# Top-k attention: the exponent moves into the evacuations, and GpSimd scales each tile behind its subtraction

## The chip, the core and the metric

The kernel runs on one core of a Trainium2 chip. Its engines work on their own and meet by semaphores: TensorE multiplies matrices (PE in the rows; PEld are its weight loads), VectorE (DVE) and ScalarE (ACT) work element by element, GpSimd (POOL) as well, and SyncE (SP) issues the transfers. The metric is the device time of one execution in microseconds, as the median of several runs.

## What is computed

Two blocks follow each other on an image of 2 x 256 x 48 x 48. The first has an attention of 8 heads of 32 channels over N = 2304 positions, in which each row of scores keeps its 64 largest:

```python
scores = jnp.einsum('bhnd,bhmd->bhnm', q, k) * DHEAD ** (-0.5)
kth = jax.lax.top_k(scores, TOPK)[0][..., -1:]
masked = jnp.where(scores >= kth, scores, jnp.finfo(scores.dtype).min)
attn = jax.nn.softmax(masked, axis=-1)
o = jnp.einsum('bhnm,bhmd->bhnd', attn, v)
```

A projection, a residual and a two-layer network with batch norms come behind it. The second block is a full attention of 8 heads over the same positions, with a projection and a residual. The change is in the first attention alone.

## The kernel before

The first attention (`attention_top`) works on tiles of 128 query rows by 2304 scores. A head has 2 images of 18 tiles; two tiles make a pair, so there are 18 pairs a head and 144 in all. Each engine has its own written program with a loop over heads, and each pair is written out in it; what stands in a program's text is its order, and semaphores are the only links between engines.

A tile goes through these steps. `score` (L366) multiplies queries and keys into PSUM; ScalarE copies the scores to SBUF (`keep_scores`, L449) into one of four slots. VectorE takes the 8 largest of each of 64 chunks of 36 scores (`chunk_tops`, L560). For a pair it then collects extremes and rests (`prepare`, L566 and L577) and finds the 64th largest of each row (`select`, L591 to L624) with the help of a first guess that ScalarE makes (`guess_place`, L480 and L483). `select` and `hand_on` of one pair are woven into the chunks of the next pair's first tile, behind chunks 7 and 19. TensorE counts rows whose threshold is in doubt (`count_doubts`, L393), ScalarE copies the count (`keep_any`, L470), VectorE loads it, searches again where it isn't zero, and hands on the threshold and the row's maximum (`give_kth`, L699 and L700).

ScalarE then writes a penalty into `probs` (`penalty`, L465): zero where a score reaches the threshold, huge where it does not. GpSimd subtracts it from the scores (L542). ScalarE exponentiates the tile in place and sums its rows into `sums` (`exponentials`, L453). TensorE transposes the tile in five groups of up to four 128 x 128 blocks (`turn`, L376) into two PSUM buffers, ScalarE copies each group to SBUF (`keep_turned`, L460), and TensorE multiplies it with the values (`weigh`, L385): 32 columns of values, so four products stand side by side in four bands of 32 rows. ScalarE copies the bands (L525), TensorE adds them up (`add_quadrants`, L404), and ScalarE stores the result (`finish`, L489). `project_out` later divides by the sums. `wait_alone` is a wait with a semaphore step of its own behind it.

## Time and profile before

| | us |
|---|---|
| median of 3 runs | 5078.21 |
| lowest and highest of them | 5076.14, 5078.52 |
| the profiled execution | 5075.16 |
| its span, first to last instruction | 5073.40 |

The profiled execution is one of the same program; its rows give the durations. Times in rows are microseconds from the start of its span, durations marked "mean ns" or "duration ns" are nanoseconds. The first attention fills the span from about 130 to 3230 us. TensorE's clock had a mean of 0.75 of its full rate in that stretch and 0.98 behind it.

### The profile page before, as it was taken

To read this page: it belongs to the slowest core of one execution; us is meant where nothing else is said; L and a number is where in the kernel's file an instruction comes from. 1 tells how busy PE (TensorE), PEld (TensorE's weight loads), DVE (VectorE), ACT (ScalarE), POOL (GpSimd) and SP (SyncE) were. 2 spreads that over 40 slices of the span, in tenths; PEclk is the share of its full clock that TensorE was granted. 3 is DMA by queue.
4 is the path that set the end of the run, shared out by engine and by line. 5 is a ranking of instruction groups with operands and counts; after the bars stand their busy time and mean duration, and the time that the engine had idled before them with its cause. 6 is when DMAs were issued, how large, how long until landed. Compare 5 with 4: busy or idle time off the path is not lost. (4 is left out here: it accounts for less than half of the span.)

```text
span 5073.4 us, 107203 instructions
## 1 busy us (share of the span) xinstructions
PE 4120.5 (81%) x32161; PEld 2777.1 (55%) x32161; DVE 4332.4 (85%) x25624; ACT 4161.6 (82%) x6082; POOL 1502.7 (30%) x362
## 2 busy tenths in 40 slices
PE   8576677777777676777777777898999999999999
PEld 4344445544555444454554445444567777777776
DVE  3999999999999999999999999431378888888886
ACT  2799799999999799999999899544268888888885
POOL 0344445444455444444444444100100000000000
PEclk9777777777777777777777777899899999999999
DMA  6000000000000000000000000200420101111112
GB/s 217 7 18 17 7 17 17 9 17 16 9 18 17 7 17 8 18 18 8 18 18 17 9 17 11 64 6 0 157 73 25 34 25 34 27 32 34 25 34 95
DMA packets 79598, 154.63 MB, mean 30 GB/s; under 512 B 8120, under 2 KB 49464, under 8 KB 73528
## 3 DMA queue, kind: packets, MB, share of 16 engines
q1 hardware_dynamic: 78904, 146.72, 10.1%
q8 instruction: 272, 4.46, 0.4%
q14 instruction: 422, 3.46, 0.2%
HBM read 99.50 MB, written 47.19 MB: 29 GB/s over the span
## 5 line engine op out<-in xcount | busy, mean ns | idle before, releaser
L542 POOL TENSOR_TENSOR a_probs<-a_scores,a_probs 128x2304 f32<-128x2304 f32 x288 | 1460.6, 5092 | 1623.8 <-ACT a_probs L465 1623.8
L560 DVE MAX8 a_top<-a_scores 128x8 f32<-128x36 f32 x18432 | 1832.5, 182 | 31.9 <-ACT a_scores L449 23.4
L376 PE MATMUL a_ps_t<-ident,a_probs 128*128 128x128 f32 x5184 | 964.0, 322 | 521.1 <-ACT a_probs_t L460 378.5
L376 PEld LDWEIGHTS a_ps_t<-ident,a_probs 128*128 128x128 f32 x5184 | 666.7, 163 | 815.0 <-ACT a_probs_t L460 519.6
L1300 DVE TENSOR_SCALAR_CACHE_REDUCE b_soft<-b_ps_s 128x2304 f32<-128x2304 f32 x288 | 735.2, 2553 | 26.2 <-PE b_ps_s L1159 8.5
L465 ACT ACTIVATE a_probs<-a_scores,a_steep_kth 128x2304 f32<-128x2304 f32 x290 | 641.3, 2212 | 136.2 <-DVE a_minus_max L700 136.1
L460 ACT ACTIVATE a_probs_t<-a_ps_t 128x512 f32<-128x512 f32 (+1 forms) x1440 | 728.9, 548 | 14.8 <-PE a_ps_t L376 3.2
L1175 PE MATMUL b_ps_t<-ident,b_soft 128*128 128x128 f32 x5184 | 727.0, 276 | 1.6 <-DVE b_soft_t L1306 0.6
L1175 PEld LDWEIGHTS b_ps_t<-ident,b_soft 128*128 128x128 f32 x5184 | 577.2, 140 | 170.1 <-ACT b_soft_t L1264 60.1
L453 ACT ACTIVATE a_probs<-a_probs,a_minus_max 128x2304 f32<-128x2304 f32 x288 | 638.1, 2216 | 31.8 <-issue 18.1
L366 PE MATMUL a_ps_s<-a_k_stack,a_q_ring 128*128 128x512 f32 (+1 forms) x1465 | 650.8, 604 | 16.1 <-ACT a_scores L449 10.7
L1257 ACT ACTIVATE b_soft<-b_soft,b_minus_max 128x2304 f32<-128x2304 f32 x288 | 638.5, 2217 | 8.2 <-DVE b_soft L1300 8.2
L449 ACT ACTIVATE a_scores<-a_ps_s 128x2304 f32<-128x2304 f32 x292 | 607.1, 2079 | 13.6 <-PE a_ps_s L366 13.6
L385 PE MATMUL a_ps_o<-a_probs_t,a_v 128*32 128x128 f32 x10368 | 568.1, 297 | 0.4
L1264 ACT ACTIVATE b_soft_t<-b_ps_t 128x512 f32<-128x512 f32 (+1 forms) x864 | 422.0, 524 | 166.4 <-PE b_ps_t L1175 166.2
L366 PEld LDWEIGHTS a_ps_s<-a_k_stack,a_q_ring 128*128 128x128 f32 x1465 | 431.3, 318 | 157.0 <-ACT a_scores L449 64.9
L1306 DVE COPY b_soft_t<-b_ps_t 128x512 f32<-128x512 f32 x576 | 393.9, 689 | 80.4 <-PE b_ps_t L1175 80.3
L1159 PE MATMUL b_ps_s<-b_k_stack,b_q_ring 128*128 128x512 f32 (+1 forms) x1440 | 442.9, 405 | 9.7 <-DVE b_soft L1300 5.0
L1136 POOL COPY b_v<-v_all 128x576 f32<-128x576 f32 x16 | 10.7, 670 | 1258.3 <-PE b_ps_o L1194 1153.8
L385 PEld LDWEIGHTS a_ps_o<-a_probs_t,a_v 128*32 128x32 f32 x10368 | 250.8, 112 | 231.8 <-issue 118.2
L404 PE MATMUL a_ps_o<-add_up,a_parts 128*128 128x32 f32 x576 | 146.5, 393 | 276.0 <-ACT a_parts L525 276.0
L1194 PE MATMUL b_ps_o<-b_soft_t,b_v 128*32 128x256 f32 x5184 | 368.4, 384 | 0.6 <-issue 0.6
(133 smaller groups left out, 4135.9 us busy)
## 6 DMA issues: line engine op xcount, KB each, us to landing
a_k_stack<-k_parts SPq DMA_DIRECT2D x72, 288.0 KB, 6.0
b_k_stack<-k_parts SPq DMA_DIRECT2D x72, 288.0 KB, 6.0
a_q_ring<-q_parts SPq DMA_DIRECT2D x294, 64.0 KB
b_q_ring<-q_parts SPq DMA_DIRECT2D x294, 64.0 KB
k_parts<-p_high SPq DMA_DIRECT2D x36, 256.0 KB, 2.0
k_parts<-p_rest SPq DMA_DIRECT2D x36, 256.0 KB, 2.1
q_parts<-p_high SPq DMA_DIRECT2D x36, 256.0 KB, 2.0
q_parts<-p_rest SPq DMA_DIRECT2D x36, 256.0 KB, 2.0
```

Source lines behind the costliest of these rows:

```text
L366: last = pe.matmul(ps_s[:, c:c + n], q_ring[pair % AHEAD_Q][:, P * (s % 2):P * (s % 2) + P], k_stack[b][:, c:c + n], start=True, stop=True)
L376: last = pe.transpose(ps_t[(NTG * s + g) % 2][:, P * m:P * m + P], probs[s % 2][:, P * (m0 + m):P * (m0 + m) + P], cst["ident"][:, :])
L385: last = pe.matmul(ps_o[rows, P * (s % 2):P * (s % 2) + P], v_s[s // MCH][:, m, :], probs_t[:, m, :], start=m < 4, stop=m + 4 >= MCH)
L449: act.activation(scores_all[:, s % 4, :], ps_s[:, 0:N], ACT.Copy).then_inc(scores_kept, 1)
L453: act.activation(probs[s % 2][:, :], probs[s % 2][:, :], ACT.Exp, scale=SCALE, bias=minus_max[parity][:, s % 2:s % 2 + 1], accum_out=sums[ ...
L460: act.activation(probs_t[:, m0:m0 + n, :], ps_t[(NTG * s + g) % 2][:, 0:n * P].rearrange("p (m q) -> p m q", q=P), ACT.Copy).then_inc(turn ...
L465: act.activation(probs[u][:, :], scores_all[:, 2 * parity + u, :], ACT.Relu, scale=-STEEP, bias=steep_kth[parity][:, u:u + 1]).then_inc(pe ...
L542: pool.tensor_tensor(probs[u][:, :], scores_all[:, 2 * (p % 2) + u, :], probs[u][:, :], ALU.subtract).then_inc(masked_ready, 1)
L560: last = dve.max(top8[s // 2 % 2][:, s % 2, c, :], scores_all[:, s % 4, CHUNK * c:CHUNK * c + CHUNK])
L1175: last = pe.transpose(ps_t[(NTG * s + g) % 2][:, P * m:P * m + P], soft[s % 3][:, P * (m0 + m):P * (m0 + m) + P], cst["ident"][:, :])
L1257: act.activation(soft[s % 3][:, :], soft[s % 3][:, :], ACT.Exp, scale=-1.0, bias=minus_max[s % 3][:, 0:1], accum_out=sums[:, s, cols(h + a ...
L1300: dve.tensor_scalar(soft[s % 3][:, :], ps_s[:, 0:N], -SCALE, None, ALU.mult, ALU.min, accum_out=minus_max[s % 3][:, 0:1]).then_inc(shifted ...
```

## The change

The whole-tile exponential (L453) is gone. In its place GpSimd, behind each subtraction, adds the row's negative maximum and multiplies by the scale in a second instruction, with a wait for the subtraction between, and the evacuation of each transposed group computes the exponential in place of a copy. The sums of rows come from TensorE: the values get 32 columns of ones beside their 32, a product has 64 columns, and two stand side by side instead of four. `add_up` has a 33rd column that picks the sum, the result tile keeps 33 columns a head, and `project_out` divides from that tile into one of its own.

The programs of TensorE and ScalarE are written in another order. A tile's groups are turned and weighed in turn; scores of tile s+5 are multiplied behind the first tile's weighing, those of s+6 within the second tile's. ScalarE keeps scores s+5 once the pair's second subtraction is done, and scores s+6 (a new place, at the end of the pair) once the next pair's first subtraction is done.

```diff
-                    rows = slice(D * (m % 4), D * (m % 4) + D)
+                    rows = slice(2 * D * (m % 2), 2 * D * (m % 2) + 2 * D)
...
-                    pe.wait_ge(probs_ready, tile + 1)
+                    pe.wait_ge(shifted_ready, tile + 1)
                     turn(s, 0, tile)
                     turn(s, 1, tile)
-                    score(s + 5, h, tile + 5)
...
+                    for g in range(2, NTG):
+                        turn(s, g, tile)
+                        weigh(s, g - 1, tile)
+                    weigh(s, NTG - 1, tile)
+                    score(s + 5, h, tile + 5)
+                    pe.wait_ge(shifted_ready, tile + 2)
                     turn(s + 1, 0, tile + 1)
-                    weigh(s, 4, tile)
+                    turn(s + 1, 1, tile + 1)
                     count_doubts(pair + 1)
...
-            def exponentials(s, h, tile, parity):
-                act.wait_ge(masked_ready, tile + 1)
-                act.activation(probs[s % 2][:, :], probs[s % 2][:, :], ACT.Exp, scale=SCALE,
-                               bias=minus_max[parity][:, s % 2:s % 2 + 1], accum_out=sums[:, s, cols(h, 1)]
-                               ).then_inc(probs_ready, 1)
...
-                               ACT.Copy).then_inc(turned_kept, 1)
+                               ACT.Exp).then_inc(turned_kept, 1)
...
-                    exponentials(s, h, tile, parity)
-                    keep_scores(s + 4, tile + 4)
+                    exponentials(s, 0, tile)
                     guess_place(1, pair + 1, 1 - parity)
...
+                    for g in range(1, NTG):
+                        exponentials(s, g, tile)
+                    wait_alone(act, masked_ready, tile + 2)
                     keep_scores(s + 5, tile + 5)
                     keep_any(pair + 1)
...
                     guess_place(0, pair + 2, parity)
+                    wait_alone(act, masked_ready, tile + 3)
+                    keep_scores(s + 6, tile + 6)
                     finish(s, h, pair)
...
                     for u in range(2):
-                        pool.wait_ge(penalty_ready, tile + u + 1)
+
+                        wait_alone(pool, penalty_ready, tile + u + 1)
                         pool.tensor_tensor(probs[u][:, :], scores_all[:, 2 * (p % 2) + u, :], probs[u][:, :],
                                            ALU.subtract).then_inc(masked_ready, 1)
+                        wait_alone(pool, masked_ready, tile + u + 1)
+                        pool.tensor_scalar(probs[u][:, :], probs[u][:, :], minus_max[p % 2][:, u:u + 1], SCALE,
+                                           ALU.add, ALU.mult).then_inc(shifted_ready, 1)
...
-                dve.tensor_scalar(minus_max[parity][:, :], extremes[:, :, 0], -SCALE, None,
+                dve.tensor_scalar(minus_max[parity][:, :], extremes[:, :, 0], -1.0, None,
                                   ALU.mult).then_inc(kth_ready, 1)
```

GpSimd, the first pair of a half head, before (`a_probs0` and `a_probs1` are the two tiles of a pair; ISA and REGISTER_ALU are steps of the sequencer):

```order
L538 COPY a_v0<-xs 128x576
L542 ISA
L542 TENSOR_TENSOR a_probs0<-a_scores,a_probs0 128x2304
L541 REGISTER_ALU
L542 TENSOR_TENSOR a_probs1<-a_scores,a_probs1 128x2304
```

and now:

```order
L536 COPY a_v0<-xs 128x18x32
L541 ISA
L541 TENSOR_TENSOR a_probs0<-a_scores,a_probs0 128x2304
L544 TENSOR_SCALAR a_probs0<-a_probs0,a_minus_max0 128x2304
L75 REGISTER_ALU
L541 TENSOR_TENSOR a_probs1<-a_scores,a_probs1 128x2304
L544 TENSOR_SCALAR a_probs1<-a_probs1,a_minus_max0 128x2304
```

Each subtraction has a scale behind it, and the second tile's subtraction comes behind the first tile's scale.

TensorE, from the first tile's last transposes to the count of the doubts, before:

```order
L376 MATMUL a_ps_t<-ident,a_probs 128x128 x2
L385 MATMUL a_ps_o<-a_probs_t,a_v 32x128 x4
L381 REGISTER_ALU
L385 MATMUL a_ps_o<-a_probs_t,a_v 32x128 x4
L430 REGISTER_ALU
L373 ISA
L376 MATMUL a_ps_t<-ident,a_probs 128x128 x4
L381 REGISTER_ALU
L385 MATMUL a_ps_o<-a_probs_t,a_v 32x128 x2
L392 REGISTER_ALU
L393 MATMUL a_ps_o<-a_doubt,ones 1x2
```

and now:

```order
L388 MATMUL a_ps_o<-a_probs_t,a_v 64x128 x4
L384 REGISTER_ALU
L388 MATMUL a_ps_o<-a_probs_t,a_v 64x128 x2
L367 REGISTER_ALU
L369 MATMUL a_ps_s<-a_k_stack,a_q_ring 128x512 x4
L369 MATMUL a_ps_s<-a_k_stack,a_q_ring 128x256
L432 REGISTER_ALU
L376 ISA
L379 MATMUL a_ps_t<-ident,a_probs 128x128 x8
L395 REGISTER_ALU
L396 MATMUL a_ps_o<-a_doubt,ones 1x2
```

The scores of tile s+5 and two groups of the second tile now stand ahead of the count; the wait at `L432` is the one for the second tile's scale.

## Rows read from the trace of the kernel before

**Rows 1.** Busy time by engine in a stretch: us, busy (instructions) each, clock, DMA.

```profile
130.00:3230.00 3100.00, 2227.86 (x18458) 1483.90 (x18459) 2936.95 (x23829) 2845.11 (x4195) 1469.74 (x303) 0.75 0.06 16
```

**Rows 2.** VectorE in order of time, one pair: start, us, engine, line, [idle before].

```profile
1514.39 0.16 DVE L700 TENSOR_SCALAR a_minus_max<-a_extremes 128x2 f32<-128x2 f32 x1
1514.46 10.58 DVE L560 MAX8 a_top<-a_scores 128x8 f32<-128x36 f32 x108
...
1527.37 0.17 DVE L591 TENSOR_SCALAR a_factor<-a_balance 128x2 f32<-128x2 f32 x1
...
1527.77 0.16 DVE L597 TENSOR_TENSOR a_eighths<-a_top 128x2 f32<-128x2 f32 x1
...
1528.68 0.80 DVE L604 SCALAR_TENSOR_TENSOR a_below<-a_top,a_guess 128x216 f32<-128x216 f32 x2
1529.40 0.16 DVE L606 TENSOR_SCALAR a_place<-a_above_guess 128x2 f32<-128x2 f32 x1
...
1534.86 0.17 DVE L699 TENSOR_SCALAR a_steep_kth<-a_kth 128x2 f32<-128x2 f32 x1 [0.42 <-issue]
1534.93 0.16 DVE L700 TENSOR_SCALAR a_minus_max<-a_extremes 128x2 f32<-128x2 f32 x1
```

**Rows 3.** ScalarE in the same pair, and its whole-tile exponentials from 130 to 3230.

```profile
1514.59 2.22 ACT L465 ACTIVATE a_probs<-a_scores,a_steep_kth 128x2304 f32<-128x2304 f32 x1 [0.30 <-DVE a_minus_max L700]
...
1524.31 2.07 ACT L449 ACTIVATE a_scores<-a_ps_s 128x2304 f32<-128x2304 f32 x1
...
L453 ACT ACTIVATE a_probs<-a_probs,a_minus_max 128x2304 f32<-128x2304 f32 x288 | 638.1, 2216 | 31.8 <-issue 18.1 <-POOL a_probs L542 9.0
```

**Rows 4.** GpSimd in order of time, the same pair.

```profile
1516.88 10.14 POOL L542 TENSOR_TENSOR a_probs<-a_scores,a_probs 128x2304 f32<-128x2304 f32 x2 [10.38 <-ACT a_probs L465]
```

**Rows 5.** L591's durations (ns, min/median/max), and two starts of half heads.

```profile
L591 DVE TENSOR_SCALAR a_factor<-a_balance x144: 149/169/304, 131.9 to 3186.5; 128x2 f32<-128x2 f32 x144
...
329.42 0.67 POOL L538 COPY a_v<-xs 128x576 f32 x1
...
329.84 0.27 DVE L591 TENSOR_SCALAR a_factor<-a_balance 128x2 f32<-128x2 f32 x1
...
3021.73 0.65 POOL L538 COPY a_v<-xs 128x576 f32 x1
...
3022.12 0.28 DVE L591 TENSOR_SCALAR a_factor<-a_balance 128x2 f32<-128x2 f32 x1
```

**Rows 6.** GpSimd's other instructions: busy us, mean ns; then two in time order.

```profile
L1016 POOL TENSOR_SCALAR m_hid<-ident,m_norm 128x128 f32<-128x128 f32 x36 | 21.0, 603 | 369.3 <-DVE m_norm L1066 369.3
...
L538 POOL COPY a_v<-xs 128x576 f32 x16 | 10.6, 662 | 111.0 <-POOLq L531 111.0
...
0.72 0.20 POOL L93 MEMSET ident<- 128x128 f32 x1 [0.29 <-POOLq L1517]
1.17 0.29 POOL L95 TENSOR_SCALAR_AFFINE_SELECT ident<-ident 128x128 f32<-128x128 f32 x1 [0.24 <-POOL ident L93]
```

**Rows 7.** TensorE in order of time around two pairs: transposes, weighing, the count.

```profile
1508.70 1.17 PE L376 MATMUL a_ps_t<-ident,a_probs 128*128 128x128 f32 x8
1509.80 0.43 PE L385 MATMUL a_ps_o<-a_probs_t,a_v 128*32 128x128 f32 x8
...
1510.80 0.65 PE L385 MATMUL a_ps_o<-a_probs_t,a_v 128*32 128x128 f32 x16
...
1512.83 0.24 PE L395 MATMUL a_ps_o<-a_doubt,ones 128*1 128x1 f32 x4
...
1524.46 1.97 PE L376 MATMUL a_ps_t<-ident,a_probs 128*128 128x128 f32 x8 [0.68 <-ACT a_probs L453]
```

**Rows 8.** L560 and L699 by line: durations in ns, first and last start, waits.

```profile
L560 DVE MAX8 a_top<-a_scores x18432: 171/180/204, 116.7 to 3184.4; 128x8 f32<-128x36 f32 x199
...
  ACT a_scores L449: 23.4, 17
...
L699 DVE TENSOR_SCALAR a_steep_kth<-a_kth x144: 169/169/172, 139.7 to 3194.0; 128x2 f32<-128x2 f32 x144
```

More of the change, by code:

```diff
@@ L84, in constants @@
         "ones": sb("ones", [P, P]),
-        "add_up": sb("add_up", [P, D]),
+        "add_up": sb("add_up", [P, D + 1]),
     }
-    made = ctx.enter_context(nc.semaphore("constants_made"))
+    made, zeroed = ctx.enter_context(nc.semaphore("constants_made")), ctx.enter_context(nc.semaphore("ident_zeroed"))
     Tally.semaphore = ctx.enter_context(nc.semaphore("waits_alone"))
@@ L92, in _ @@
         def _(pool):
-            pool.memset(k["ident"][:, :], 0.0).then_inc(made, 1)
-            pool.wait_ge(made, 1)
+            pool.memset(k["ident"][:, :], 0.0).then_inc(zeroed, 1)
+            pool.wait_ge(zeroed, 1)
             pool.affine_select(out=k["ident"][:, :], in_=k["ident"][:, :], compare_op=ALU.not_equal,
                                fill=1.0, base=0, pattern=[[-1, P]],
-                               channel_multiplier=1).then_inc(made, 1)
+                               channel_multiplier=1).then_inc(made, 2)
         @block.vector
@@ L101, in _ @@
             dve.memset(k["ones"][:, :], 1.0)
-            dve.wait_ge(made, 2)
-            for quadrant in range(4):
-                rows = slice(D * quadrant, D * quadrant + D)
-                dve.tensor_copy(k["add_up"][rows, :], k["ident"][rows, rows])
+            dve.memset(k["add_up"][:, :], 0.0).then_inc(made, 1)
+            dve.wait_ge(made, 3)
+            for half in range(2):
+                values, total = 2 * D * half, 2 * D * half + D
+                dve.tensor_copy(k["add_up"][values:values + D, 0:D], k["ident"][values:values + D, values:values + D])
+                dve.tensor_copy(k["add_up"][total:total + D, D:D + 1], k["ident"][total:total + D, total:total + 1])
     return k
@@ L283, in attention_top @@
                                                operands.q_loaded)
-        v_s = [sb(f"v{n}", [P, MCH, D]) for n in range(2)]
+        v_s = [sb(f"v{n}", [P, MCH, 2 * D]) for n in range(2)]
         scores_all = sb("scores", [P, 4, N])
@@ L403, in add_quadrants @@
                 for u in range(2):
-                    last = pe.matmul(ps_o[:, O_COL + D * u:O_COL + D * u + D], parts[:, P * u:P * u + P],
+                    first = O_COL + (D + 1) * u
+                    last = pe.matmul(ps_o[:, first:first + D + 1], parts[:, P * u:P * u + P],
                                      cst["add_up"][:, :], start=True, stop=True)
@@ L449, in keep_scores, with exponentials @@
                 act.activation(scores_all[:, s % 4, :], ps_s[:, 0:N], ACT.Copy).then_inc(scores_kept, 1)
-            def exponentials(s, h, tile, parity):
-                act.wait_ge(masked_ready, tile + 1)
-                act.activation(probs[s % 2][:, :], probs[s % 2][:, :], ACT.Exp, scale=SCALE,
-                               bias=minus_max[parity][:, s % 2:s % 2 + 1], accum_out=sums[:, s, cols(h, 1)]
-                               ).then_inc(probs_ready, 1)
-            def keep_turned(s, g, tile):
+            def exponentials(s, g, tile):
                 m0, n = TGROUPS[g]
@@ L498, in _ @@
             act.wait_ge(kth_ready, 1)
-            for u in range(2):
-                penalty(u, 0)
+            penalty(0, 0)
+            penalty(1, 0)
             guess_place(0, 1, 1)
+            act.wait_ge(masked_ready, 1)
+            keep_scores(4, 4)
             with act.Fori(0, HEADS) as h:
@@ L504, in _ @@
                     pair, tile, s, parity = h * HEAD_PAIRS + p, h * HEAD_TILES + 2 * p, 2 * p, p % 2
-                    exponentials(s, h, tile, parity)
-                    keep_scores(s + 4, tile + 4)
+                    exponentials(s, 0, tile)
                     guess_place(1, pair + 1, 1 - parity)
-                    keep_turned(s, 0, tile)
-                    keep_turned(s, 1, tile)
-                    exponentials(s + 1, h, tile + 1, parity)
-                    keep_turned(s, 2, tile)
-                    keep_turned(s, 3, tile)
-                    keep_turned(s, 4, tile)
+                    for g in range(1, NTG):
+                        exponentials(s, g, tile)
+                    wait_alone(act, masked_ready, tile + 2)
                     keep_scores(s + 5, tile + 5)
                     keep_any(pair + 1)
-                    keep_turned(s + 1, 0, tile + 1)
-                    keep_turned(s + 1, 1, tile + 1)
+                    exponentials(s + 1, 0, tile + 1)
+                    exponentials(s + 1, 1, tile + 1)
                     act.wait_ge(kth_ready, pair + 2)
                     penalty(0, 1 - parity)
-                    keep_turned(s + 1, 2, tile + 1)
-                    keep_turned(s + 1, 3, tile + 1)
-                    keep_turned(s + 1, 4, tile + 1)
+                    for g in range(2, NTG):
+                        exponentials(s + 1, g, tile + 1)
                     penalty(1, 1 - parity)
@@ L531, in _ @@
             pool.sem_inc(weighed, MCH + 1)
+            for n in range(2):
+                pool.memset(v_s[n][:, :, D:2 * D], 1.0).then_inc(ones_set, 1)
+            pool.wait_ge(ones_set, 2)
             with pool.Fori(0, HEADS) as h:
@@ L767, in load, with project_out @@
         sync.dma_start(self.bias[:, :], bias).then_inc(self.w_loaded, 16)
[L770 removed]
+def project_out(nc, cst, xs, o_top, projection):
     CW = BANK
```

53 lines of the change are left out of this document (24 added, 29 removed).

## The prediction

> **What bounds the kernel now.** I read the stretches first. The top-k attention runs from about 130 to 3230 us, and the diff touches almost nothing else; VectorE is busy 2937 of its 3100 us, ScalarE 2845, TensorE 2228, GpSimd 1470 [rows 1]. Two engines are close to full, so the next view is one pair of tiles on VectorE in order of time [rows 2]. Call t = 0 the end of L700, where VectorE hands over the thresholds (1514.39 + 0.16 = 1514.55). The next L700 ends at 1535.09: the pitch is **20.54 us**, and the only idle time in it is the 0.42 us before L699. ScalarE on the other hand waits in every pair, 0.30 us before its first penalty, and for L700 [rows 3]. So VectorE sets the pitch and ScalarE follows it closely. Over the whole run VectorE's MAX8 waited for ScalarE's scores in 17 places, 23.4 us in all [rows 8]; that is all that a faster ScalarE can give back there. L699 comes 144 times from 139.7 to 3194.0 [rows 8], a mean pitch of 21.36 over 143 steps; the 0.82 over 20.54 are the pairs whose threshold VectorE searches again. That part stays as it is, so what the change does to the regular pitch counts 143 times.
>
> GpSimd is what I look at last. It subtracts two tiles in 10.14 us and then idles 10.38 [rows 4]. Its work ends at 1516.88 + 10.14 = 1527.02, and VectorE's selection begins with L591 at 1527.37, 0.35 us later [rows 2]. The whole selection, L591 to L700, lies in GpSimd's idle time. At 15 of the 16 places where a new half head begins GpSimd is not idle there, since it copies the values (L538). The first and last of the 15 are in [rows 5]: the copy runs 329.42 to 330.09 and L591, started at 329.84, ends at 330.11; it runs 3021.73 to 3022.38 and L591 of 3022.12 ends at 3022.40. L591 has 2 columns and takes 169 ns in the median, but 304 at most. **It is held until GpSimd's instruction has ended**, and finishes some 0.02 us behind it. MAX8 is not: beside GpSimd or not, all 18432 lie between 171 and 204 ns [rows 8].
>
> **The change part by part.** *ScalarE* loses 288 whole-tile exponentials, 638.1 us [rows 3], some 4.4 us a pair, and computes the exponent in the ten evacuations that it makes anyway. I cost this at nothing: VectorE sets the pitch, and the saving is covered by its work. The 23.4 us above are the most it can give.
>
> *TensorE* weighs with 64 columns in place of 32, so two products run side by side instead of four. Eight records take 0.43 us and sixteen 0.65 [rows 7]; a group of four products, eight records now side by side in two rounds, takes four rounds in the new form, so 0.22 more; 4.5 groups a tile make that 1.0 us, 2 us a pair, on an engine that is idle 28% of this stretch. Hidden, but it lies in a loop of the third rival.
>
> *The new waits of ScalarE.* Scores of tile s+6 now follow the next pair's first subtraction (below: t = 7.40) and take 2.07 us as they do now [rows 3]. VectorE wants them eight MAX8 before L591, at 12.82 - 8 x 0.098 = 12.0 [rows 2], so some 2.5 us are left. Scores of tile s+5 wait for the second subtraction; queued behind are the copy of the doubt flags and the next evacuations, and VectorE wants the flags only after its selection. Both hidden. The row of ones, the longer `add_up` and the division from a strided tile happen once, outside the loop: nothing.
>
> *GpSimd* gets a scale (L544 of the new file) behind each subtraction, with a wait for that subtraction between. Its price **X** isn't in the trace. The same operation on 128 columns is 603 ns, a copy of 576 columns 662 [rows 6]. Taking the first as start and the copy's 1.149 ns for each further element: 603 + 2176 x 1.149 = **3.10 us**, which I take, since it keeps the operation's own row. From below: if the copy starts like the memset (0.20 for 128 columns), each element is (662 - 200) / 448 = 1.03 ns and X = 0.20 + 2176 x 1.03 = 2.44. From above: no dearer than the two-input subtraction, 5.07. A GpSimd instruction that waits for the one ahead starts 0.24 us behind it (L95) [rows 6].
>
> Now the pair again, from t = 0. GpSimd starts at 1516.88, t = 2.33; the first subtraction ends at 7.40, its scale at 7.64 + X, the second subtraction at **12.71 + X**, and the second scale runs from 12.95 + X to **12.95 + 2X**. VectorE's own work doesn't change, so L591 is due at 1527.37, t = 12.82, in the middle of the second subtraction for any X over 0.11. It is held to 12.73 + X. That is 3.0 us lost. L594 slips in behind it; L597, 0.23 us behind L591's end, comes to 12.96 + X, a hundredth behind the second scale's start. The next step with two SBUF inputs is L604, 0.91 us after L597 [rows 2], and that surely meets the scale. The trace shows no two-input step beside GpSimd; bounds are MAX8 (not held) and L591 (held to the end). I take held, since L594, L597 and L591 are the same 2 columns on the same memory. Of L597 and L604 I take L604, because the new wait has one more sequencer step than the one at L95 had. So L604 starts at 12.97 + 2X, and from there to L700's end is 1535.09 - 1528.68 = 6.41 [rows 2]:
> pitch = 12.97 + 2X + 6.41 = 19.38 + 2X = **25.58** with X = 3.10, or 5.04 more than now. 143 x 5.04 = 721 us. The profiled execution took 5075.16 in all (span 5073.40); 5075.16 + 721 = 5796, and 3 more since the median of the runs lies 3 above it: **5800**. Were L597 held already, it is 0.91 more a pair, 130 us: 5930.
>
> The Trainium skill ("SBUF — State Buffer", section "Who interferes with whom") states the two-input case: such a VectorE instruction contends with a GpSimd instruction that reads SBUF, and whichever started first keeps the port for the whole instruction. L591 agrees with the second half (ended 0.02 us behind the copy); the first half no run here shows. By the page the forecast's sum holds, without it the second rival's, 5696.
>
> **The rivals.**
> 1. *A cheaper scale.* X = 2.44, all else as above: pitch 24.26, 143 x 3.72 = 532, so 5610. For it: it is one-input work like the copy. Against: 603 ns for 128 columns. The Trainium skill ("GPSIMD Engine Reference", section "Engine selection") calls one-input work roughly line-rate there; an estimate from its 1.2 GHz is 1.92 us, and the sum would give 5464.
> 2. *Two-input steps aren't held, the tensor_scalar form is.* L591 to 12.73 + X as above, then L606 1.9 us later, which has L591's form and waits for 12.97 + 2X; from it to L700's end 5.69. Pitch 18.66 + 2X = 24.86: 143 x 4.32 = 618, so 5075 + 618 + 3 = 5696.
> 3. *Nothing is held for long; a loop through GpSimd sets the pitch.* In the new order TensorE counts the doubts of a pair behind the second scale and two groups of transposes, so thresholds lead to penalty, both subtractions and scales, transposes (1.17 or 1.97 us for eight, by stretch), count 0.24 [rows 7], VectorE's 0.42 and 0.23 [rows 2]: 12.95 + 2X + 2.06 = 15.01 + 2X, or 15.81 + 2X, hand-overs not counted. With X = 3.10 that is 21.21 to 22.01, 96 to 210 us more: 5174 to 5288. Against: L591's 15 places.
> 4. *The other side: the pitch stays VectorE's.* As 3, with X under 2.37 to 2.77, from where the loop is shorter than 20.54. Then VectorE's 23.4 us of waiting for scores [rows 8] go as well: 5055. It needs both that the hold fails and the cheap scale; if only part of the 23.4 goes, nothing can be told.
> 5. *A scale as dear as the subtraction*, 5.07: pitch 29.52, 143 x 8.98 = 1284, so 6362.
>
> **How the numbers follow.** Chances: forecast 0.44, cheap scale 0.20, tensor_scalar alone held 0.13, the loop 0.09, the other side 0.07, dear scale 0.07. The likeliest is 5800. The range reaches from 5250 (the upper part of the loop case) to 6200 (X = 4.5 in the forecast's sum); left out are the other side, half of the loop case and most of the dear scale, some 0.18. A measurement of this kernel can tell about 0.2% from no change. Slower takes everything but case 4: 0.93; of case 4 0.05 falls to faster and 0.02 to no difference.
>
> **What would show it.** In the profile after: L700 to L700 25.6 us in a pair without a second search; L591 some 3 us long (or idle ahead of it) and ending with a subtraction; L604 starting where the second scale ends; MAX8 unchanged; the scale near 3.1 us; ScalarE busy about 4.4 us less a pair and waiting for L700. Wrong would be L591 at 0.17 us beside a running subtraction (cases 3 and 4: then the idle time before L699 is put down to ScalarE's flags, or there is none), L604 and L597 at their present distances with only L606 held (case 2), or a scale well off 3.1, of which each 0.1 us moves the time by 29.

## The result, and the profile after

The changed kernel takes **5529.2 us** (median of 4 runs, 5525.4 to 5531.2), the kernel before beside it 5078.4 (4 runs): a ratio of **1.089**, 95% interval 1.0876 to 1.0902. It is 451 us slower. The forecast was 5800 with a range of 5250 to 6200; the time lies in the range, 271 us under the forecast.

The top-k attention now runs to about 3670 us, 440 us further. This is its stretch by engine (us, then busy time and instructions of TensorE, its weight loads, VectorE, ScalarE and GpSimd, then the granted clock), the counterpart of [rows 1]:

```profile
130.00:3670.00 3540.00, 2519.84 (x18436) 1820.70 (x18435) 3317.99 (x23813) 2263.65 (x3601) 2100.53 (x591) 0.79 0.05 14
```

ScalarE is busy 2264 us in place of 2845, so the exponentials are gone from it as intended. VectorE is busy 381 us more, though the change gave it no work. Where those went is in the groups by line (busy us, mean ns of one, then the idle time of the engine ahead of them). The lines moved by four: L595, L608, L703 of the new file are L591, L604 and L699 of the old one.

```profile
L564 DVE MAX8 a_top<-a_scores 128x8 f32<-128x36 f32 x18432 | 1831.1, 180 | 37.4 <-issue 21.3 <-ACT a_scores L450 14.5
L595 DVE TENSOR_SCALAR a_factor<-a_balance 128x2 f32<-128x2 f32 x144 | 274.5, 1906 | 28.9 <-ACT a_compared L479 27.9
L608 DVE SCALAR_TENSOR_TENSOR a_below<-a_top,a_guess 128x216 f32<-128x216 f32 x288 | 261.7, 947 | 5.2
L604 DVE TENSOR_SCALAR_CACHE_REDUCE a_below<-a_top,a_guess 128x216 f32<-128x216 f32 x288 | 113.7, 432 | 0.0
L703 DVE TENSOR_SCALAR a_steep_kth<-a_kth 128x2 f32<-128x2 f32 x144 | 24.4, 169 | 86.9 <-issue 71.7 <-ACT a_any_doubt L466 14.4
...
L544 POOL TENSOR_SCALAR a_probs<-a_probs,a_minus_max 128x2304 f32<-128x2304 f32 x288 | 631.2, 2192 | 59.3 <-POOL a_probs L541 59.3
```

An instruction of two columns takes 1.9 us in the mean. The same groups of the kernel before are these:

```profile
L560 DVE MAX8 a_top<-a_scores 128x8 f32<-128x36 f32 x18432 | 1832.5, 182 | 31.9 <-ACT a_scores L449 23.4 <-issue 1.7
L604 DVE SCALAR_TENSOR_TENSOR a_below<-a_top,a_guess 128x216 f32<-128x216 f32 x288 | 114.9, 440 | 5.2
...
L591 DVE TENSOR_SCALAR a_factor<-a_balance 128x2 f32<-128x2 f32 x144 | 25.8, 179 | 3.6 <-issue 2.5 <-ACT a_compared L483 1.0
L699 DVE TENSOR_SCALAR a_steep_kth<-a_kth 128x2 f32<-128x2 f32 x144 | 24.4, 169 | 62.1 <-issue 58.6 <-ACT a_any_doubt L470 1.6
```

Five of their differences add up to the loss:

| place | before | after | us more |
|---|---|---|---|
| L595 (L591), busy | 25.8 | 274.5 | 248.7 |
| L608 (L604), busy | 114.9 | 261.7 | 146.8 |
| idle ahead of L703 (L699) | 62.1 | 86.9 | 24.8 |
| idle ahead of L595 (L591) | 3.6 | 28.9 | 25.3 |
| idle ahead of L564 (L560) | 31.9 | 37.4 | 5.5 |
| sum | | | 451.1 |

Two instructions that were stretched carry 395 of the 451 us. That the five match the loss so closely is chance, since VectorE's other work in the stretch is 14 us shorter, and 13 us of the longer span lie outside the stretch. One pair in order of time shows what stretched them, first GpSimd (start, us, engine, line):

```profile
1523.22 5.08 POOL L541 TENSOR_TENSOR a_probs<-a_scores,a_probs 128x2304 f32<-128x2304 f32 x1 [8.61 <-ACT a_probs L461]
1528.51 2.19 POOL L544 TENSOR_SCALAR a_probs<-a_probs,a_minus_max 128x2304 f32<-128x2304 f32 x1 [0.21 <-POOL a_probs L541]
1530.66 5.08 POOL L541 TENSOR_TENSOR a_probs<-a_scores,a_probs 128x2304 f32<-128x2304 f32 x1
1535.94 2.19 POOL L544 TENSOR_SCALAR a_probs<-a_probs,a_minus_max 128x2304 f32<-128x2304 f32 x1 [0.21 <-POOL a_probs L541]
```

and VectorE in the same pair, from one hand-over (L704) to the next:

```profile
1520.62 0.16 DVE L704 TENSOR_SCALAR a_minus_max<-a_extremes 128x2 f32<-128x2 f32 x1
...
1533.49 2.27 DVE L595 TENSOR_SCALAR a_factor<-a_balance 128x2 f32<-128x2 f32 x1
...
1535.99 0.16 DVE L601 TENSOR_TENSOR a_eighths<-a_top 128x2 f32<-128x2 f32 x1
...
1536.90 1.82 DVE L608 SCALAR_TENSOR_TENSOR a_below<-a_top,a_guess 128x216 f32<-128x216 f32 x2
...
1544.06 0.17 DVE L703 TENSOR_SCALAR a_steep_kth<-a_kth 128x2 f32<-128x2 f32 x1 [0.38 <-issue]
1544.14 0.16 DVE L704 TENSOR_SCALAR a_minus_max<-a_extremes 128x2 f32<-128x2 f32 x1
```

The second subtraction ends at 1530.66 + 5.08 = 1535.74, L595 at 1533.49 + 2.27 = 1535.76. The second scale ends at 1538.13; L608, begun at 1536.90, is there for 1.82 us, where its two instructions took 0.80 in [rows 2]. The pitch of this pair is 1544.30 - 1520.78 = 23.52 us; over all pairs L703 comes from 137.8 to 3639.4, a mean of 24.49 against 21.36, and 143 x 3.13 = 447 us.

### The profile page after: what moved, and what is told of

Same layout as the page of the kernel before. It is cut to its first block and busy times, and to the rows that moved or that the text cites. A ratio compares the mean times of both kernels' runs of the same rounds, so it can differ in the third digit from the quotient of the medians.

```text
span 5526.7 us, 107489 instructions
## 1 busy us (share of the span) xinstructions
PE 4420.7 (80%) x32161; PEld 3120.5 (56%) x32161; DVE 4721.7 (85%) x25625; ACT 3587.5 (65%) x5507; POOL 2134.6 (39%) x652
## 5 line engine op out<-in xcount | busy, mean ns | idle before, releaser
L564 DVE MAX8 a_top<-a_scores 128x8 f32<-128x36 f32 x18432 | 1831.1, 180 | 37.4 <-issue 21.3
L388 PE MATMUL a_ps_o<-a_probs_t,a_v 128*64 128x128 f32 x10368 | 1072.4, 342 | 305.0 <-ACT a_probs_t L456 303.3
L456 ACT ACTIVATE a_probs_t<-a_ps_t 128x512 f32<-128x512 f32 (+1 forms) x1440 | 774.6, 549 | 737.6 <-PE a_ps_t L379 735.2
L379 PE MATMUL a_ps_t<-ident,a_probs 128*128 128x128 f32 x5184 | 1053.3, 344 | 223.0 <-POOL a_probs L544 199.6
L388 PEld LDWEIGHTS a_ps_o<-a_probs_t,a_v 128*64 128x64 f32 x10368 | 691.2, 168 | 615.5 <-ACT a_probs_t L456 382.9
L379 PEld LDWEIGHTS a_ps_t<-ident,a_probs 128*128 128x128 f32 x5184 | 723.6, 174 | 464.3 <-POOL a_probs L544 214.4
L544 POOL TENSOR_SCALAR a_probs<-a_probs,a_minus_max 128x2304 f32<-128x2304 f32 x288 | 631.2, 2192 | 59.3 <-POOL a_probs L541 59.3
L369 PE MATMUL a_ps_s<-a_k_stack,a_q_ring 128*128 128x512 f32 (+1 forms) x1465 | 468.0, 459 | 13.3 <-ACT a_scores L450 8.9
L369 PEld LDWEIGHTS a_ps_s<-a_k_stack,a_q_ring 128*128 128x128 f32 x1465 | 311.0, 230 | 93.7 <-issue 35.0
L408 PE MATMUL a_ps_o<-add_up,a_parts 128*128 128x33 f32 x576 | 95.4, 291 | 272.8 <-ACT a_parts L518 272.8
```

The costliest lines, as they stand in the source:

```text
L369: last = pe.matmul(ps_s[:, c:c + n], q_ring[pair % AHEAD_Q][:, P * (s % 2):P * (s % 2) + P], k_stack[b][:, c:c + n], start=True, stop=True)
L379: last = pe.transpose(ps_t[(NTG * s + g) % 2][:, P * m:P * m + P], probs[s % 2][:, P * (m0 + m):P * (m0 + m) + P], cst["ident"][:, :])
L388: last = pe.matmul(ps_o[rows, P * (s % 2):P * (s % 2) + P], v_s[s // MCH][:, m, :], probs_t[:, m, :], start=m < 2, stop=m + 2 >= MCH)
L456: act.activation(probs_t[:, m0:m0 + n, :], ps_t[(NTG * s + g) % 2][:, 0:n * P].rearrange("p (m q) -> p m q", q=P), ACT.Exp).then_inc(turne ...
L544: pool.tensor_scalar(probs[u][:, :], probs[u][:, :], minus_max[p % 2][:, u:u + 1], SCALE, ALU.add, ALU.mult).then_inc(shifted_ready, 1)
L564: last = dve.max(top8[s // 2 % 2][:, s % 2, c, :], scores_all[:, s % 4, CHUNK * c:CHUNK * c + CHUNK])
```

## The experiments

Theory H (hold): VectorE's steps with L591's form, and those with two SBUF inputs, stand still while GpSimd works; the pitch is 19.38 + 2X. Rival L (loop): thresholds, penalties, GpSimd, TensorE and the doubt flags form a loop of which the scale is one part. Nine kernels ran; each row is the median of its runs against the kernel before on the same chip.

| kernel | us | ratio, 95% interval |
|---|---|---|
| after | 5529.2 | 1.089 (1.0876 to 1.0902) |
| e1: after, no scale | 5293.0 | 1.043 (1.0408 to 1.0443) |
| e2: after, scale on half the columns | 5321.4 | 1.048 (1.0456 to 1.0498) |
| e3: before, plus an unread scale | 5305.7 | 1.045 (1.0425 to 1.0467) |
| e4: before, plus an unread memset | 5274.1 | 1.038 (1.0363 to 1.0405) |
| e5: e1, scores of s+5 early | 5092.8 | 1.003 (1.0019 to 1.0040) |
| e6: after, scores of s+5 early | 5495.4 | 1.082 (1.0804 to 1.0837) |
| e7: before, plus two unread memsets | 5137.4 | 1.012 (1.0100 to 1.0131) |
| e8: e5, counting on ScalarE | 5025.3 | 0.989 (0.9876 to 0.9909) |
| e9: e8, doubts counted earlier | 4947.6 | 0.974 (0.9729 to 0.9755) |

### e3 and e4: is it the hold?

Both add one instruction to GpSimd in the kernel *before*, behind each pair's second subtraction, on a tile that nobody reads; nothing else waits for it.

```diff
+                    wait_alone(pool, idle_set, h * HEAD_PAIRS + p + 2)
+                    pool.tensor_scalar(idle[:, :], idle[:, :], nought[:, 0:1], 1.0,
+                                       ALU.add, ALU.mult).then_inc(idle_set, 1)
```

> The kernel before with one more GpSimd instruction behind each pair's second subtraction: the same scale on a tile of its own that nobody reads and nobody waits for. It runs from about t = 12.5 to 14.7. Theory of the hold: L591, due at 12.82, ends at 14.7, and 7.55 us of VectorE's work follow; pitch 22.26, 1.72 more, total 5078 + 246 = 5324. Rival (only waits by semaphores matter): nothing waits for it, so 5078.

In e4 the last two lines are `pool.memset(idle[:, :], 0.0).then_inc(idle_set, 1)`.

> As the run with the idle scale, but GpSimd writes the tile with a memset of the same 2304 columns, which reads nothing. Estimated at 1.9 us from the rows of 0.10 us for one column and 0.20 for 128. If any GpSimd instruction holds a tensor_scalar of VectorE, L591 is held to about t = 14.4: pitch 22.0, total about 5285. If only those that read the memory hold it: 5078.

Measured: 5305.7 and 5274.1, 18 and 11 us under the hold's sums. GpSimd's added instruction and L591 (L597 in e3's file, L596 in e4's), in e3

```profile
1517.09 2.19 POOL L548 TENSOR_SCALAR a_idle<-a_idle,a_nought 128x2304 f32<-128x2304 f32 x1
...
1517.45 1.86 DVE L597 TENSOR_SCALAR a_factor<-a_balance 128x2 f32<-128x2 f32 x1
...
L597 DVE TENSOR_SCALAR a_factor<-a_balance 128x2 f32<-128x2 f32 x144 | 243.6, 1692 | 4.1 <-issue 2.6 <-ACT a_compared L484 1.5
```

and in e4:

```profile
1504.85 2.02 POOL L548 MEMSET a_idle<- 128x2304 f32 x1
...
1505.26 1.64 DVE L596 TENSOR_SCALAR a_factor<-a_balance 128x2 f32<-128x2 f32 x1
```

The first ends at 1519.28 and L597 at 1519.31; the second at 1506.87 and L596 at 1506.90. In e3 there is no new dependence at all, and 227 us are lost; L597 alone is busy 243.6 us in place of 25.8, 218 us more. That shows the hold as a cause, not only as something seen beside the loss. e4 shows that it needs no reading: an instruction that only writes holds L591 too.

### e7: which of VectorE's forms does a write-only instruction hold?

The kernel before with two memsets, the second long enough to lie beside L597 to L606 of [rows 2].

```diff
+                    wait_alone(pool, idle_set, 2 * (h * HEAD_PAIRS + p) + 2)
+                    pool.memset(idle[:, 0:N // 2], 0.0).then_inc(idle_set, 1)
+                    wait_alone(pool, idle_set, 2 * (h * HEAD_PAIRS + p) + 3)
+                    pool.memset(idle[:, 0:N], 0.0).then_inc(idle_set, 1)
```

> The kernel before, with two memsets of an unread tile on GpSimd behind each pair's second subtraction, of 1152 and then 2304 columns, the second waiting for the first. The first ends about 0.6 us behind the moment at which L591 (2 columns, tensor_scalar) is due, the second begins 0.2 us later and lasts 2.0. Theory A (a write-only GpSimd instruction holds two-input VectorE steps too): L604's first comes 0.7 us into the second memset and ends with it, about 1.3 us late; pitch 1.8 us longer, 5310 to 5340. Theory B (it holds the tensor_scalar form alone, and two-input steps only beside GpSimd instructions that read): L604 keeps its 0.44 us, and L606, of L591's form, is held some 0.6 us; 5210 to 5240.

Measured: 5137.4. One pair of e7, GpSimd and then VectorE (L591, L594, L597, L604, L606 are L598, L601, L604, L611, L613 here):

```profile
1511.99 1.06 POOL L548 MEMSET a_idle<- 128x1152 f32 x1
1513.20 2.02 POOL L550 MEMSET a_idle<- 128x2304 f32 x1 [0.15 <-POOL a_idle L548]
...
1512.40 0.67 DVE L598 TENSOR_SCALAR a_factor<-a_balance 128x2 f32<-128x2 f32 x1
...
1513.30 0.16 DVE L604 TENSOR_TENSOR a_eighths<-a_top 128x2 f32<-128x2 f32 x1
...
1514.22 0.80 DVE L611 SCALAR_TENSOR_TENSOR a_below<-a_top,a_guess 128x216 f32<-128x216 f32 x2
1514.93 0.32 DVE L613 TENSOR_SCALAR a_place<-a_above_guess 128x2 f32<-128x2 f32 x1
...
1515.07 0.67 DVE L619 MAX8 a_best<-a_below 128x8 f32<-128x216 f32 x2
```

L611, with two SBUF inputs, runs from 1514.22 to 1515.02 wholly within the memset (1513.20 to 1515.22) at its old 0.80 us. L613, the form of L591, is held and ends 0.03 us behind the memset. So theory B: write-only work on GpSimd holds the tensor_scalar form, and not the steps with two SBUF inputs (L604, of 2 columns, keeps its 0.16 us too). In the kernel after, the scale reads SBUF, and L608 was held. The 5137 lie under B's 5210. L598 is held 0.50 us, and the median pitch is 0.47 us longer (21.02 against 20.55). The hold of L613, 0.16 us where 0.6 was expected, costs nothing: the next MAX8 (L619) begins 0.14 us behind L613's start, as L612 does behind L606's in the kernel before.

The Trainium skill ("SBUF — State Buffer", section "Who interferes with whom") says that a two-input VectorE instruction contends with GpSimd instructions that read SBUF, not with those that only write it, and counts tensor_scalar without an accumulator among the forms that can contend with either. The rows agree: the first L608 of a pair takes 1.46 us beside the scale (the mean of both is 947 ns), L611 0.80 us for two beside the memset, L604 (with accumulator) 432 ns in the kernel after. One row stands apart: L601 of the kernel after has two SBUF inputs, begins 0.05 us behind the start of the scale (1535.99 and 1535.94) and still takes 0.16 us.

### e1 and e2: the scale taken away, and halved

e1 leaves the whole-tile scale out: ScalarE's exponential multiplies by the scale itself, and the shift by the row's maximum is dropped, which the division by the sums cancels.

```diff
-                               ACT.Exp).then_inc(turned_kept, 1)
+                               ACT.Exp, scale=SCALE).then_inc(turned_kept, 1)
...
-                        wait_alone(pool, masked_ready, tile + u + 1)
-                        pool.tensor_scalar(probs[u][:, :], probs[u][:, :], minus_max[p % 2][:, u:u + 1], SCALE,
-                                           ALU.add, ALU.mult).then_inc(shifted_ready, 1)
```

> The changed kernel without the scale instruction: the factor sits in the evacuations' exponent (scale = SCALE), the row's maximum is not subtracted, which leaves the softmax the same; TensorE waits for the subtraction. Everything else of the change stays (64-column weighing, new order, sums by ones). Theory of the hold: the second subtraction ends at t = 12.5, before VectorE's first selection step is due at 12.82, so nothing is held; pitch 20.5 us, total 5055 to 5085. Rival (the loss lies in TensorE's wider weighing, in the new order or in ScalarE's new waits): these are all still there, so most of the 451 us stays, 5400 to 5530.

Measured: 5293.0, **neither theory**. The groups in e1 (L591, L604, L699 are L592, L605, L700):

```profile
L605 DVE SCALAR_TENSOR_TENSOR a_below<-a_top,a_guess 128x216 f32<-128x216 f32 x288 | 114.8, 440 | 5.1
L592 DVE TENSOR_SCALAR a_factor<-a_balance 128x2 f32<-128x2 f32 x144 | 44.6, 310 | 1.3 <-ACT a_compared L479 1.1
L700 DVE TENSOR_SCALAR a_steep_kth<-a_kth 128x2 f32<-128x2 f32 x144 | 24.4, 170 | 265.7 <-issue 190.5 <-ACT a_any_doubt L466 74.7
```

The hold is all but gone (L605 at its old 440 ns). But VectorE now idles 265.7 us ahead of the hand-over, 203.6 more than before: a second cause lay behind the first. One pair of e1 along it, from VectorE's hand-over over GpSimd, TensorE and ScalarE to the next:

```profile
1520.48 0.16 DVE L701 TENSOR_SCALAR a_minus_max<-a_extremes 128x2 f32<-128x2 f32 x1
...
1523.08 10.10 POOL L541 TENSOR_TENSOR a_probs<-a_scores,a_probs 128x2304 f32<-128x2304 f32 x2 [12.47 <-ACT a_probs L461]
...
1528.20 1.50 PE L379 MATMUL a_ps_t<-ident,a_probs 128*128 128x128 f32 x8 [0.26 <-POOL a_probs L541]
...
1536.35 0.98 PE L388 MATMUL a_ps_o<-a_probs_t,a_v 128*64 128x128 f32 x12
1537.27 1.33 PE L369 MATMUL a_ps_s<-a_k_stack,a_q_ring 128*128 128x512 f32 x5
...
1538.63 2.09 ACT L450 ACTIVATE a_scores<-a_ps_s 128x2304 f32<-128x2304 f32 x1 [1.79 <-PE a_ps_s L369]
1540.62 0.14 ACT L466 ACTIVATE a_any_doubt<-a_ps_o 1x3 f32<-1x3 f32 x1
...
1541.46 0.17 DVE L700 TENSOR_SCALAR a_steep_kth<-a_kth 128x2 f32<-128x2 f32 x1 [1.15 <-ACT a_any_doubt L466]
```

The hand-over before this pair ended at 1520.64. From there to TensorE's first transpose, through a penalty and the first subtraction, are 7.56 us; TensorE turns and weighs the whole first tile until 1537.27 (9.07); the scores of tile s+5, now behind that, are ready for ScalarE at 1538.63 (1.36); it copies them (1.99), and only then the doubt flags, for which VectorE waits; L700 begins 0.84 later and the hand-over ends 0.24 after that, at 1541.70. Together 21.06 us, 0.5 more than VectorE's own pitch. This is one of the shortest pairs of e1: the median pitch is 22.05, and 42 of the 132 pitches without a second search take 23.0 us or more. The granted clock is 0.84 in this pair and 0.78 in the one ahead of it, which takes 23.00 us; more of TensorE's work runs there at the lower of its two clock levels (eight weighings take 1.12 us in place of 0.66).

e2 scales only the first 1152 columns of each tile, the rest stays unscaled.

```diff
-                        pool.tensor_scalar(probs[u][:, :], probs[u][:, :], minus_max[p % 2][:, u:u + 1], SCALE,
+                        pool.tensor_scalar(probs[u][:, 0:N // 2], probs[u][:, 0:N // 2], minus_max[p % 2][:, u:u + 1], SCALE,
```

> The changed kernel with the scale on the first 1152 of 2304 columns (the other half is left unscaled, so the outputs are not the reference's). The scale should take about 1.34 us in place of 2.19 (0.58 for 128 columns, 0.74 ns for each further one). Theory of the hold: the pitch holds twice the scale, so it falls by 2 x 0.85 from 23.52 to 21.8; 5529 - 143 x 1.70 = 5286. Rival (a loop through GpSimd and TensorE of 15.0 to 15.8 us plus two scales sets the pitch): 18 us is under VectorE's 20.54, so about 5080; and if the loss has nothing to do with the scale, 5529.

Measured: 5321.4. The scale takes 1.228 us:

```profile
L544 POOL TENSOR_SCALAR a_probs<-a_probs,a_minus_max 128x1152 f32<-128x1152 f32 x288 | 353.7, 1228 | 59.3 <-POOL a_probs L541 59.3
...
L703 DVE TENSOR_SCALAR a_steep_kth<-a_kth 128x2 f32<-128x2 f32 x144 | 24.4, 170 | 143.5 <-issue 108.9 <-ACT a_any_doubt L466 34.1
```

The 5321.4 are 35 us over the 5286 of the hold, and VectorE idles 143.5 us ahead of the hand-over, in place of 86.9 in the kernel after: the loop has a part in it. The hold's sum is 19.38 + 2 x 1.23 = 21.84; the loop of e1's pair with one half scale and its 0.21 of waiting is 21.06 + 1.44 = 22.50. Of the 132 pitches without a second search, 67 have under 0.55 us of idle time ahead of L703, about as before, and a median of 21.60; the other 65 idle longer, with a median of 22.98. So in e2 the hold sets about half of the pitches and the loop the other half. In the kernel after, the two sums are 23.76 and 21.06 + 2.40 = 23.46; there 90 pitches have the usual idle time and a median of 23.52, which is the hold, and 42 idle longer, with a median of 24.32. The loop's sums start from one of e1's shortest pairs, so they are estimates and on the low side. What the two causes cost can't be added up, since in the kernel after both contain the scale.

### e5 and e6: the second loop opened, without and with the scale

Both move the scores of tile s+5 back to where they stood, behind the first tile's first two groups, and ScalarE's copy of them between the third and the fourth evacuation.

```diff
                     turn(s, 1, tile)
+                    score(s + 5, h, tile + 5)
...
                     weigh(s, NTG - 1, tile)
-                    score(s + 5, h, tile + 5)
...
-                    for g in range(1, NTG):
+                    for g in range(1, 3):
                         exponentials(s, g, tile)
                     wait_alone(act, masked_ready, tile + 2)
                     keep_scores(s + 5, tile + 5)
+                    for g in range(3, NTG):
+                        exponentials(s, g, tile)
```

> The changed kernel without the scale (the whole-tile scale on GpSimd is left out, the exponential takes no shift, which a softmax does not need), and TensorE's and ScalarE's order changed in one respect: the scores of tile s+5 are multiplied right behind the first tile's first two groups of transposes, as in the kernel before, and ScalarE keeps them between the third and the fourth evacuation of the first tile, so that its copy of the doubt flags no longer stands right behind a score that TensorE makes late. Theory (without the scale nothing is held, and the 210 us that are left come from ScalarE's flags standing behind keep_scores of s+5): the pitch falls back to VectorE's 20.5 us, VectorE's wait ahead of the hand-over from 1.15 to 0.5 us or less, the time from 5293 to 5055 to 5085. Rival (the loss is in TensorE's longer weighing and in its clock, wherever the score stands): 5270 to 5300, wait unchanged.

> The changed kernel with its scale, and the same reorder of the scores of tile s+5. Theory (with the scale VectorE is held by GpSimd and the flags are in time, so the second loop has slack): the pitch stays at 23.3 to 23.5 us, the time at 5490 to 5530, at most the 27 us of VectorE's waits for flags and balances come back. Rival (the order of the scores is the larger loss also with the scale): 5270 to 5350.

Measured: e5 5092.8, e6 5495.4. In e5 the wait ahead of the hand-over falls from 265.7 to 105.5 us:

```profile
L594 DVE TENSOR_SCALAR a_factor<-a_balance 128x2 f32<-128x2 f32 x144 | 36.4, 253 | 1.2 <-ACT a_compared L479 1.2
...
L702 DVE TENSOR_SCALAR a_steep_kth<-a_kth 128x2 f32<-128x2 f32 x144 | 24.4, 170 | 105.5 <-issue 89.7 <-ACT a_any_doubt L466 15.5
```

So 200 of e1's 214 us were that order, TensorE's and ScalarE's part of it together. e5 ends 0.3% above the kernel before, a little over its 5055 to 5085: the wait stays 43 us above the 62 of before. The rest of the change, ScalarE's 638 us of saved exponentials with it, brings no time. With the scale in place (e6) the same move gives back 34 us, somewhat more than the 27 expected, and the hold is as it was, with a median pitch of 23.54 in both kernels; now only 3 of the 132 pitches have the longer idle time, in place of 42:

```profile
L597 DVE TENSOR_SCALAR a_factor<-a_balance 128x2 f32<-128x2 f32 x144 | 318.8, 2214 | 3.9 <-ACT a_compared L479 2.4
L610 DVE SCALAR_TENSOR_TENSOR a_below<-a_top,a_guess 128x216 f32<-128x216 f32 x288 | 266.0, 962 | 5.1
```

VectorE reaches L597 earlier and stands there longer: 318.8 us in place of 274.5.

One pair of e6 shows what becomes of L601 of the kernel after (L603 here) when it comes later than 0.05 us into the scale:

```profile
1901.49 2.20 POOL L546 TENSOR_SCALAR a_probs<-a_probs,a_minus_max 128x2304 f32<-128x2304 f32 x1 [0.21 <-POOL a_probs L543]
...
1901.72 1.98 DVE L603 TENSOR_TENSOR a_eighths<-a_top 128x2 f32<-128x2 f32 x1
```

Its 2 columns take 1.98 us, to the scale's end. Five times in e2 and e6 a step of 2 columns with two SBUF inputs began 0.075 to 0.223 us behind a scale's start, and each was held to the scale's end. Over 400 times in the kernel after, e2 and e6 one began 0.044 to 0.055 us behind it, and none of these was held.

### e8 and e9: using ScalarE's free time

In e5 ScalarE idles over a quarter of the stretch from 130 to 3240 us, while VectorE is busy 2917 of its 3110 us. e8 moves work from the one to the other: ScalarE counts the candidates above the guess, by the sum of their signs, VectorE loses its two counting steps, the row's maximum (no longer needed without the shift) and half of the reduction for it. It also puts ScalarE's copy of the scores of tile s+5 behind the first tile's last evacuation, right ahead of the doubt flags again.

```diff
+                for u in range(2):
+                    act.activation(signs[:, u, :, :], top8[parity][:, u, :, 0:KEEP], ACT.Sign, scale=-1.0,
+                                   bias=guess[:, u:u + 1], accum_out=balance_above[:, u:u + 1]).then_inc(above_ready, 1)
...
-                for u in range(2):
-                    rows = counted(dve.tensor_scalar(below_of(u), candidates(u), guess[:, u:u + 1], None, ALU.is_ge,
-                                                     ALU.add, accum_out=above_guess[:, u:u + 1]))
-                after(rows)
```

> The kernel of e5 (no scale, early scores), in which the time that ScalarE has gained is used: ScalarE counts the candidates above the guess (Sign with an accumulator, two instructions a pair, behind the second evacuation of the first tile) in place of VectorE's two counting steps, VectorE no longer computes the row's negative maximum, and reduces one extreme a chunk in place of two. ScalarE keeps the scores of tile s+5 behind the first tile's last evacuation. Theory (VectorE's work sets the pitch of e5, 20.7 us in the median): it loses 0.84 us of counting, 0.07 of L703 and about 0.3 of the reduction; the loop through GpSimd, some 19.7 us, is next; pitch 19.6 to 19.9, so 0.8 to 1.1 us less than in e5, 4935 to 4985, faster than both kernels. Rival (the loop through GpSimd, TensorE and ScalarE already sets the pitch of e5): the work taken from VectorE comes back as idle time ahead of L702, and the time stays at 5070 to 5100.

Measured: 5025.3, between the two theories. Of some 1.2 us taken from VectorE in each pair (174 us in all), 66 us came back as idle time ahead of L711, the hand-over, which is 171.7 us in place of 105.5, and 19 us ahead of L610. One pair shows why, TensorE, ScalarE and VectorE:

```profile
1506.03 1.09 PE L381 MATMUL a_ps_t<-ident,a_probs 128*128 128x128 f32 x8
1507.05 0.19 PE L398 MATMUL a_ps_o<-a_doubt,ones 128*1 128x2 f32 x2
...
1505.50 2.09 ACT L452 ACTIVATE a_scores<-a_ps_s 128x2304 f32<-128x2304 f32 x1
1507.47 0.14 ACT L468 ACTIVATE a_any_doubt<-a_ps_o 1x3 f32<-1x3 f32 x1
...
1505.73 0.16 DVE L636 SCALAR_TENSOR_TENSOR a_doubt<-a_beyond,a_kth 128x2 f32<-128x2 f32 x1
...
1508.63 0.17 DVE L711 TENSOR_SCALAR a_steep_kth<-a_kth 128x2 f32<-128x2 f32 x1 [1.56 <-issue]
```

The row's "issue" is time that the profile puts down to no instruction; VectorE must load the flags and branch on them. It has the doubts at 1505.89, but TensorE counts them behind two groups of transposes, at 1507.05, and ScalarE copies scores until 1507.47. e9 takes both out of the way; the two moves were not tried apart.

```diff
                     weigh(s, NTG - 1, tile)
+                    count_doubts(pair + 1)
                     pe.wait_ge(masked_ready, tile + 2)
                     turn(s + 1, 0, tile + 1)
                     turn(s + 1, 1, tile + 1)
-                    count_doubts(pair + 1)
...
                     exponentials(s, 1, tile)
-                    count_above(pair + 1, 1 - parity)
-                    for g in range(2, NTG):
-                        exponentials(s, g, tile)
                     wait_alone(act, masked_ready, tile + 2)
                     keep_scores(s + 5, tile + 5)
+                    exponentials(s, 2, tile)
+                    count_above(pair + 1, 1 - parity)
+                    for g in range(3, NTG):
+                        exponentials(s, g, tile)
```

> The kernel of e8 with two moves. TensorE counts the doubts right behind the first tile's last weighing, ahead of the second tile's two groups of transposes (1.09 us). ScalarE keeps the scores of tile s+5 behind the first tile's second evacuation, counts above the guess behind its third, and so has nothing long left ahead of the copy of the doubt flags. Theory (in e8 the loop through TensorE's transposes and ScalarE's keep_scores sets the pitch, with 1.55 us of idle time ahead of VectorE's hand-over in most pairs): that idle time falls to 0.4 to 0.7 us, the median pitch from 20.47 to 19.3 to 19.7, the time from 5025 to 4880 to 4930. Rival (TensorE's own work at the lower of its two clock levels sets the pitch): the wait goes to another place and the time stays at 5000 to 5030.

Measured: **4947.6 us**, 2.6% under the kernel before (0.9729 to 0.9755), 10.5% under the kernel after. The idle time is back at the level of before; L604, which is L591, is held again, since VectorE now reaches it before GpSimd's second subtraction has ended:

```profile
L604 DVE TENSOR_SCALAR a_factor<-a_balance 128x2 f32<-128x2 f32 x144 | 59.9, 416 | 2.9 <-ACT a_compared L481 2.8
L712 DVE TENSOR_SCALAR a_steep_kth<-a_kth 128x2 f32<-128x2 f32 x144 | 24.4, 169 | 68.4 <-issue 67.2
```

The median pitch is 19.68, at the upper end of what was expected; the time is 18 us above its range, and the holds, (416 - 179) x 144 = 34 us, are what the expectation hadn't counted.

## Why the prediction was right in direction and too high

- **The scale's price X was mis-sized.** 3.10 us was taken, 2.44 to 5.07 were the bounds; it is 2.19, under the lower bound too. The 3.10 and the 2.44 both took a start from one operation and a price per element from the copy, 1.15 and 1.03 ns. The scale pays (2192 - 1228) / 1152 = 0.84 ns an element, which no row of before showed. By the sum's own rule, 29 us for each 0.1 us, the 0.91 us are 0.91 x 286 = 260 of the 271 us that the forecast was too high. The Trainium skill ("GPSIMD Engine Reference", section "Engine selection") calls one-input work roughly line-rate; the 1.92 estimated from it was 0.27 us too low, about as far off as the 2.44, which was 0.25 too high. (By the sum's rule 1.92 gives 5461, not 5464.)
- **L591 held to the subtraction's end** (forecast: 0.02 us behind it): right. 1535.74 and 1535.76, and e3 shows that it is the cause.
- **L597 slips through, L604 is held to the second scale's end**: right (L601 0.16 us, L608 1.82 us for two), the first by luck. The scale was to begin behind L597 because of its longer wait; it begins 0.05 us ahead of L601, which is L597, and L601 still slips through. A few hundredths of a microsecond later it would have been held, as e6's pair shows, at the price of 0.91 us a pair that the prediction gives. That two-input steps are held was taken without a row; rival 2, only L606's form held, has fallen for a GpSimd instruction that reads, and e7 shows that it does hold for one that only writes.
- **The pitch, 19.38 + 2X**: 23.76 with the measured X against 23.52. Of the 0.24, 0.21 are L608's: the sum lets it start at the scale's end, but the two end 0.59 us behind the scale (1538.13 to 1538.72), where 0.80 was counted, as if the held instruction had a part of its time behind it when it is let go.
- **GpSimd's times within the pair**: the second scale's end was put at t = 12.95 + 2X = 17.33; it is 1538.13 - 1520.78 = 17.35.
- **ScalarE's saving at nothing, VectorE's 23.4 us as the most to gain**: the first is borne out by e5. Of the 23.4, 14.5 are left in the kernel after, but ahead of L564 VectorE idles 37.4 us in all, more than the 31.9 of before.
- **Rival 3, the loop, was put on the wrong path and too short.** It was led through both subtractions and both scales to the count, 15.0 + 2X, which is 19.4 us with the measured X. The longer path goes through the first tile's weighing, then score(s+5), which the change had moved behind it, and ScalarE's queue: 21.06 us without any scale in a short pair of e1, and only one X on it, some 23.5 us. The step that failed is the one on ScalarE's new waits: it has the copy of s+5 wait for the second subtraction only, not for the score, which now came later, and so calls the flags queued behind it hidden. It did little harm to the sum, and that was luck: the hold happened to be the longer of the two in 90 of 132 pitches, and undoing the order with the scale in place gives back 34 us (e6). For the same reason rival 4, that without a hold VectorE's pitch stays, was no real case: e1 gives 5293, not 5055.

A chance of 0.93 for slower was right in its mechanism. What was left unsaid is that this diff holds two causes, and that either is enough to make the kernel 4 to 8% slower: e1 has almost only the loop, without a scale in it (1.043), e6 almost only the hold (1.082). No run takes the hold away and leaves the scale in the loop. What sets the length of the loop in the pairs of 22 to 23 us of e1, beyond the lower clock seen there, was not tried apart.

## What to carry to other kernels

Work given to an idle GpSimd isn't free where VectorE runs steps with two SBUF inputs or plain tensor_scalar beside it: look for which VectorE instructions fall into GpSimd's new busy time, and count the hold to the *end* of GpSimd's instruction, whatever the VectorE step's size. When a multiplication is moved on TensorE's program, follow what waits for it on the next engine and what is queued behind that wait; a flag of 0.14 us behind a copy that waits for a late score cost 200 us without the scale and 34 with it. And time freed on an engine that doesn't set the pitch was worth something here only when work of the engine that does was moved there (e8), with the flags cleared from behind long work (e9).

## What the runs showed of the hardware

- A tensor_scalar of 128 x 2 on VectorE waits for the end of the GpSimd instruction that is running: copy, two-input subtraction, scale and write-only memset, all that were tried, held it, and it ended 0.02 to 0.03 us behind them in the pairs shown. Unexpected was the memset.
- A VectorE step with two SBUF inputs (216 columns) is held by GpSimd's scale, which reads (1.46 us for the first of a pair), and not by its memset, which only writes (0.80 us for two). A two-input step of 2 columns that began 0.05 us behind the scale's start slipped through (0.16 us); one that began 0.22 us behind it in e6 was held to the end (1.98 us). The copy that GpSimd makes at the start of a half head holds L608 as well (0.84 us in 15 places of the kernel after). In the kernel after, MAX8 (180 ns), tensor_scalar with an accumulator (432 ns) and GpSimd's own subtraction (5.08 us) kept their times.
- GpSimd's one-input tensor_scalar with two operations takes 1.23 us for 1152 columns and 2.19 for 2304; a memset takes 1.07 and 2.02; the two-input subtraction of 2304 takes 5.08. The memset, which reads nothing, is hardly cheaper than the scale.
